# Attention scores on 64-row tiles of the array: one head pair per tile, masks moved to GpSimd, one ring of four banks

## What is computed

```
x = x + LN(attn(LN(x)))          # 16 heads of 8 features, causal, ALiBi bias
    scores = q k^T * 8**-0.5 + slope[h] * (i - j);  scores = where(i >= j, scores, -inf)
    out = softmax(scores) @ v @ Wo + bo
x = x + LN(ffn(LN(x)))
    ffn(x): x = x + LN1(attn(x))  # the same size, no mask, no bias
            x = x + LN2(moe(x))   # 8 experts, 2 chosen of each token, hidden 512, gelu
```

## Time and profile before

| | us |
|---|---|
| median of 3 runs | 2289.57 |
| lowest and highest run | 2287.91, 2292.93 |
| profiled execution, first to last instruction | 2287.5 |

### The profile page before, as it was taken

One profiled execution on the slowest core, in us unless ns is written; L12 is line 12 of the kernel. 1 busy time (PEld: TensorE's weight loads), 2 busy tenths in 40 slices (PEclk: granted clock), 3 DMA queues, 4 the chain that ended last, 5 costly groups with the idle time before them and its releaser, 6 DMA issues. The chain is left out here.

```text
span 2287.5 us, 41083 instructions
## 1 busy us (share of the span) xinstructions
PE 2102.9 (92%) x11100; PEld 1223.1 (53%) x11100; DVE 1671.8 (73%) x3157; ACT 1373.5 (60%) x2647; POOL 977.3 (43%) x744
## 2 busy tenths in 40 slices
PE   5899999999999679999999999999993999999996
PEld 4455555555554534555555555555531666666664
DVE  5766667666672787777777777778822899998986
ACT  4266566666666616666666666666672655555654
POOL 3665464553610355333333333342002466565554
PEclk7799999999999679999999999999996999999998
DMA  2000000000000300000000000000001100000000
GB/s 59 1 2 1 3 1 1 2 2 1 1 1 2 110 0 1 2 1 1 2 1 1 2 1 1 1 1 1 1 1 61 51 19 19 2 19 19 19 10 10
DMA packets 27508, 24.96 MB, mean 11 GB/s; under 512 B 2409, under 2 KB 21110, under 8 KB 27282
## 3 DMA queue, kind: packets, MB, share of 16 engines
q1 hardware_dynamic: 26400, 21.91, 3.2%
q10 hardware_dynamic: 882, 0.36, 0.1%
HBM read 13.87 MB, written 6.29 MB: 9 GB/s over the span
## 5 line engine op out<-in xcount | busy, mean ns | idle before, releaser
L466 DVE TENSOR_REDUCE at_mx<-at_a 128x1 f32<-128x512 f32 (+3 forms) x1632 | 1010.8, 675 | 358.7 <-PE at_a L333 249.5
L415 ACT ACTIVATE at_probs<-at_b 128x512 f32<-128x512 f32 (+3 forms) x1792 | 888.6, 558 | 474.0 <-PE at_b L360 292.7
L333 PE MATMUL at_a<-at_km,at_fq 128*128 128x512 f32 (+1 forms) x1632 | 704.8, 439 | 20.4 <-DVE at_mx L466 9.8
L360 PE MATMUL at_b<-at_fqm,at_km 128*128 128x512 f32 (+3 forms) x1792 | 710.8, 404 | 11.4 <-ACT at_probs L415 7.6
L333 PEld LDWEIGHTS at_a<-at_km,at_fq 128*128 128x128 f32 x1632 | 316.3, 194 | 290.0 <-DVE at_mx L466 224.4
L360 PEld LDWEIGHTS at_b<-at_fqm,at_km 128*128 128x128 f32 x1792 | 339.8, 191 | 205.5 <-ACT at_probs L415 120.3
L378 PE MATMUL at_pv<-at_probs,at_vst 128*32 128x512 f32 (+3 forms) x3584 | 437.9, 561 | 1.5 <-ACT at_probs L415 1.5
L556 POOL TENSOR_TENSOR at_hi<-at_u,split_sign 128x512 fp32r<-128x512 f32 x120 | 124.9, 1041 | 441.1 <-ACT at_u L404 306.5
L1172 ACT ACTIVATE t_hid<-t_bank_h,b1t 128x512 f32<-128x512 f32 x256 | 174.3, 689 | 195.9 <-DVE t_hid_lo L1306 113.1
L1306 DVE TENSOR_TENSOR t_hid_lo<-t_hid,t_hid_hi 128x512 fp32r<-128x512 f32 x256 | 225.6, 917 | 15.0 <-ACT t_hid_hi L1179 11.8
L569 POOL TENSOR_TENSOR at_km<-at_fk,head_mask 128x2048 fp32r<-128x2048 f32 x60 | 216.1, 3602 | 11.2 <-POOL at_fk L567 11.0
(11 more groups left out here) (211 smaller groups left out, 2410.3 us busy)
## 6 DMA issues: line engine op xcount, KB each, us to landing
t_raw<-L_ffn_W SPq DMA_DIRECT2D x16, 256.0 KB, 3.1
x_first<-L_attn_x SPq DMA_DIRECT2D x4, 512.0 KB, 7.3
second_x_in<-L_attn_x SPq DMA_DIRECT2D x8, 256.0 KB, 3.1
kept<-second_joined SPq DMA_DIRECT2D x8, 256.0 KB, 2.6
kept_u<-second_normed SPq DMA_DIRECT2D x8, 256.0 KB, 2.0
t_heads_in<-tokens SPq DMA_DIRECT2D x8, 256.0 KB, 2.6
t_u_in<-kept_u SPq DMA_DIRECT2D x8, 256.0 KB, 3.1
t_x_in<-kept SPq DMA_DIRECT2D x8, 256.0 KB, 3.1
```

The lines of the kernel that those rows point to most:

```text
L333: mm = pe.matmul(scores, fq[g][:, qt * P:(qt + 1) * P], km[g][:, heads[0]:heads[0] + k, kh * HALF:kh * HALF + w], start=True, stop=not dia ...
L360: mm = pe.matmul(out[:, 0:w], km[g][:, j, kt * P:(kt + 1) * P], fqm[g % 2][:, q0:q0 + w], start=True, stop=not diagonal)
L415: act.activation(probs[(t % 2) * GH + j][:, 0:w], b_bank[n % 3][:, 0:w], ACT.Exp).then_inc(exp_done, 1)
L466: dve.tensor_reduce(mx[:, kh, qt, heads[0]:heads[0] + k], a_bank[n % 3][:, 0:k * w].rearrange("p (k w) -> p k w", k=k), AX.X, ALU.max).the ...
```

## The change

- Keys: `km` has two layers instead of four. Rows 0 to 63 belong to heads 0 and 1, rows 64 to 127 to heads 2 and 3; layer j % 2 has only head j's 32 rows nonzero, in its half. The tiles are cleared once in the first block; after that `fk` (now two buffers) is copied in by four DMAs of 32 partitions x 512 columns a half, issued by SP. The product with `head_mask` goes.
- `a` and `b` matmuls contract over the 64 rows of the head's pair. `b` takes the heads in the order 0, 2, 1, 3, and so do chunks of one head; chunks have at most two heads (in at1 40 chunks a slot instead of 38; at2 keeps 64).
- The causal mask: for `a` two matmuls of 64 rows each (`half_ident`, `half_mask`) instead of one of 128; for `b` none, POOL sets the upper triangle of the four exponentials to zero after the fact (`affine_select`), and `pv` waits for it (`masked`).
- Order of a step: first `b`, all `a`, the other three `b`, then as before. `lead` is 3; `pv` is that of the quad two before.
- Banks: `a`, `proj`, `otr` and `mtr` share one ring of four banks in the order of the list; `b` keeps three and `pv` one. `probs` holds four quads instead of two.

```diff
+RING = ("a", "proj", "otr", "mtr")
+A_BANKS = 4
+B_BANKS = 3
+PROBS = 4
+B_HEADS = (0, 2, 1, 3)
+PAIR = 2 * HW
...
-                per = max(1, HALF // n)
-                per = 4 if per >= 4 else per
-                for j in range(0, GH, per):
+                per = 2 if n <= HALF // 2 else 1
+                for j in (0, 2) if per == 2 else (0, 2, 1, 3):
...
-        self.lead = 2
-        a_steps = nq - 4
+        self.lead = 3
+        a_steps = nq - 2 - self.lead
...
-            out += self.interleave(bs, ass)
+            out += bs[:1] + ass + bs[1:]
...
-            dp, p = (ds, q - 1) if q else (0, self.nq - 1)
+            dp, p = (0, i + 1) if i + 1 < self.nq else (1, 0)
...
-                        scores = out[:, 0:k * w].rearrange("p (k w) -> p k w", k=k)
-                        mm = pe.matmul(scores, fq[g][:, qt * P:(qt + 1) * P],
-                                       km[g][:, heads[0]:heads[0] + k, kh * HALF:kh * HALF + w],
+                        scores = misc[:, 0:k * w].rearrange("p (k w) -> p k w", k=k)
+                        rows = slice(PAIR * (heads[0] // 2), PAIR * (heads[0] // 2 + 1))
+                        first = heads[0] % 2
+                        mm = pe.matmul(scores, fq[g][rows, qt * P:(qt + 1) * P],
+                                       km[g][rows, first:first + k, kh * HALF:kh * HALF + w],
                                        start=True, stop=not diagonal)
                         if diagonal:
-                            mm = pe.matmul(scores[:, :, w - P:w], ident16[:, :],
-                                           causal_mask[:, None, :].broadcast_to([P, k, P]),
-                                           start=False, stop=True)
+                            for i in range(2):
+                                mm = pe.matmul(scores[:, :, w - P:w], half_ident[rows, i, :],
+                                               half_mask[rows, i, None, :].broadcast_to([PAIR, k, P]),
+                                               start=False, stop=(i == 1))
...
-                        out = b_bank[n % 3]
-                        mm = pe.matmul(out[:, 0:w], km[g][:, j, kt * P:(kt + 1) * P],
-                                       fqm[g % 2][:, q0:q0 + w], start=True, stop=not diagonal)
-                        if diagonal:
-                            mm = pe.matmul(out[:, 0:P], causal_mask[:, :], ident16[:, :],
-                                           start=False, stop=True)
+                        out = b_bank[n % B_BANKS]
+                        rows = slice(PAIR * (j // 2), PAIR * (j // 2 + 1))
+                        mm = pe.matmul(out[:, 0:w], km[g][rows, j % 2, kt * P:(kt + 1) * P],
+                                       fqm[g % 2][rows, q0:q0 + w], start=True, stop=True)
...
+                        if n in plan.diagonals:
+                            done(pe, masked, len(plan.diagonals), s, plan.diagonals.index(n))
...
+                    if what == "b" and n % GH == GH - 1 and n // GH in plan.diagonals:
+                        await_(exp_done, NB, s, n)
+                        block_ = probs[n // GH % PROBS][:, :, 0:P]
+                        pool.affine_select(block_, block_, [[0, GH], [1, P]], ALU.is_ge, 0.0, base=0,
+                                           channel_multiplier=-1).then_inc(masked, 1)
...
+                    if m:
+                        await_(keys_spread[h], KEYS, s - 1, KEYS - 1)
+                    dst = fk[h][:, :] if m else fq[g][:, half]
+                    pool.tensor_tensor(dst, part[:, :], un[:, :], ALU.add).then_inc(split_done, 1)
...
+        @block.sync
+        def _(sp):
...
+                    if ds == 3 and n == 0:
+                        done(sp, b_made, NB, s - 4, NB - 1)
+                    done(sp, split_done, 4, s, n)
+                    for j in range(GH):
+                        rows = slice(HW * j, HW * (j + 1))
+                        sp.dma_start(km[g][rows, j % 2, h * HALF:(h + 1) * HALF].bitcast(F32),
+                                     fk[h][rows, :].bitcast(F32)).then_inc(keys_spread[h], 16)
```

More of the change, by code:

```diff
@@ L76, in __init__ @@
                 self.quads.append((qh, kt))
+        self.diagonals = [t for t, (qh, kt) in enumerate(self.quads) if causal and kt * P >= qh * HALF]
         self.na = len(self.chunks)
@@ L135, in body, with places @@
         return out
+    def places(self, steps):
+        order = [step for step in steps if step[0] in RING]
+        return {step: place for place, step in enumerate(order)}
     def prologue(self):
@@ L247, in attention @@
         dve_step = sem("dve_step")
+        keys_spread = [sem(f"keys_spread{i}") for i in range(2)]
         v_staged = sem("v_staged")
@@ L288, in _, with emit, bank_free @@
                 pe.sem_inc(semaphore, per)
-            def emit(steps, s0, b0, g0):
-                prologue = steps[0][0] == "proj" and steps[0][1] == 0
-                before = None if prologue else ("otr", -1, 1)
+            def emit(steps, s0, b0, g0, places, before):
+                prologue = places is in_prologue
+                held = list(places)
+                emitted = (set(steps), set(before))
+                def bank_free(step):
+                    place = places[step] - A_BANKS
+                    while True:
+                        back = 0 if place >= 0 else 1
+                        if prologue and back:
+                            return
+                        what, ds, n = held[place]
+                        if held[place] in emitted[back]:
+                            break
+                        place -= A_BANKS
+                    s = s0 + (ds - back)
+                    if what == "a":
+                        done(pe, a_read, NA, s, n)
+                    elif what == "proj":
+                        done(pe, proj_read, 4, s, n)
+                    elif what == "otr":
+                        done(pe, o_done, 2, s, n)
+                    else:
+                        done(pe, fqm_made, 2, s, n)
                 for what, ds, n in steps:
                     s = s0 + ds
[L295 to L307, removed]
+                    if what in RING:
+                        bank_free((what, ds, n))
+                        misc = a_bank[places[what, ds, n] % A_BANKS]
                     if what == "proj":
@@ L1516, in gpsimd @@
                 pool.memset(row3[:, :, :, :, :], 0.0).then_inc(zeroed, 1)
+                for i in range(2):
+                    pool.memset(km[i][:, :, :].bitcast(F32), 0.0).then_inc(cleared, 1)
                 pool.wait_ge(zeroed, 1)
```

144 lines of the change are left out of this document (76 added, 68 removed).

## The result

The changed kernel takes 2211.99 us in the median (2207.67 to 2218.02, 4 runs), the kernel before 2288.74 beside it (2287.1 to 2292.93): a ratio of 0.9668, 95% interval 0.9647 to 0.9689. That is 77 us less, where 219 were forecast. The time lies above the forecast's range of 1975 to 2182 us. The page after: span, busy time, the slices of PE and of its clock, three of its groups, and the DMA that is new.

What follows compares the result with a forecast made beforehand. PE was taken to bound both attention stages. From 2287.5 us, 94.5 (at2), 112.5 (at1), 10 (starts) and 3 (last slots) came off, giving 2067.5, so 2070 us as the median; range 1975 to 2182 us.

Steps and rivals of the forecast that it cites:

- Overlap of the halves: Score matmuls on 64 rows: two row halves overlap fully, 13.1 us a slot less in at2, 7.6 in at1.
- Loads one after another: Rival for score matmuls: halves overlap in streaming, but each waits for its own weight load; 2160 us, chance 0.17.
- doesn't do what it says: Rival: a half of the rows runs no sooner than the whole array; 2287 us, no change, chance 0.08.
- drains: Rival for score matmuls: going between halves empties the array, 0.09 us each, no overlap remains; 2495 us, chance 0.05.
- Who is late next in at2: At2 slots: PE (42.0 us) and DVE (42.5) become equal and coupled through four banks; 48.1 us a slot, gain 94.5.
- the forecast's chain of 2.54 us: At2, from a step's last chunk to the next step's first chunk result; leaves DVE idle 0.15 us a step.
- Its last sentence: At2: a chain through the banks longer than 2.54 us would break the sum even with overlap; DVE's idle time shows it.
- at1: Causal attention stage: PE still sets the slot, 33.5 us instead of 41.0, gain 112.5 us.
- POOL: At1 triangle selections: 1.3 us each, covered, 23.1 us of POOL a slot; rival at 3.6 us each 2182, chance 0.10.
- Starts and last slots: Stage starts lose two key products on DVE, 10 us less; last slots lose 3 us over 26 steps.
- the bare 0.32: Last slots: time from fourth score to values falls from 0.43 to 0.32 us, 3 us less over 26 steps.
- The granted clock is no case of its own: PE's clock in the last slot: 1.00 of 2.4 GHz though PE waits there; no longer waits expected, so no separate rival.

Runs made afterwards that it cites:

- the later turns: Both turns of the row maxima one step later in the slot, against the kernel with values in halves (2131.98 us): 2160.48 us, ratio 0.9449.
- the added matmuls: Changed kernel with extra half-row matmuls into idle banks in the last slot's steps: 2204.98 us with two from the fifth quad on, 2207.19 with four from the first step.

## Where the forecast failed, and what of it was right

- **Overlap of the halves: right.** Five starts in 0.6 us, loads in pairs, no price for going from one half to the other. "Loads one after another", "doesn't do what it says" and "drains" all fall with the timeline after and with the 245 us by which the halved values are slower without overlap. By the Trainium skill, TensorEngine Tiling (Array Packing), "Key Properties", a change of the tile alone doesn't drain TensorE; the prediction could compare that for columns only, and for rows this trace agrees (1311.03, both halves start together). The streaming gain was put at 7.6 and 13.1 us a slot; where nothing hides it, it is 6.4 and 11.1.
- **Who is late next in at2: the step that failed.** The forecast put 48.1 us a slot, from DVE's work plus 0.15 us of idle time a step (2.55 us); measured 52.45. Two terms were missing.
  - The wait of the fourth "b" for its bank, put at nothing. In the forecast's chain of 2.54 us the last chunk of a step is followed by the values after 0.23 + 0.46 + 0.09 = 0.78 us. Measured it is 1.13 (1311.59 to 1312.72): 0.70 until the fourth "b", whose bank ACT has to read first, and 0.43 until the values. The next step's first chunk starts with its first "b", which gives 0.22 back. That makes 2.69 us for each step, 16 x 0.14 = 2.2 us a slot. With four banks for "b" the wait is gone, and a shorter exponential shortens it by as much.
  - The uneven chunks, which make long steps that short ones don't repay: 2.2 us, the gain of the even ones.

48.1 + 2.2 + 2.2 = 52.5. With both mended the slot took the forecast's 48.1, but in an order of steps that the forecast had not summed, so this equality is in part luck. The chain was in the earlier trace rows, and the forecast used it for the last slot alone, though a burst of "b" on a faster PE meets the same three banks in every slot. Its last sentence looked for a longer chain through the ring and DVE, not through ACT. The Trainium skill, TensorEngine Tiling (Array Packing), "PSUM Bottleneck", says that tiling quickens TensorE but not the emptying of PSUM. That pointed the right way; but here the banks' readers bound by their delay before they were full (DVE 82% busy). The prediction also read a plain step of the kernel before as 2.9 us, where it takes 3.05; as its sums start from whole slots, this changed none of them.

- **at1: right in kind, too low.** 33.5 us forecast, 36.0 in a regular slot, 36.8 with the boundaries. The forecast let PE work without a pause, and took no wait into account. PE had none before. Over three regular slots of the changed kernel it has, first its busy time and then one of the waits:

```profile
133.50:241.40 107.90, 101.99 (x790) 53.21 (x788) 81.37 (x150) 71.92 (x162) 56.17 (x64) 1.00 0.07 16
```

```profile
PE at_a L381 <- DVE at_mpad L513: 3.1, 3, 1.0
```

So 2.0 of the 2.5 us that are missing are idle time, half of it before the turns, which wait for the padded maxima, and most of the rest before "b". Moving the fourth matmul and shortening the exponential gain 0.9 and 0.8 us in a regular slot of at1, so the chain through ACT costs something there too; the even chunks and the halved values bring nothing (36.4 both). Which count the last 0.5 us belong to is open.

- **POOL: right.** 0.634 us a selection, half of the 1.3 taken; the value matmuls waited for it once, 1.7 us, and 6.2 us of idle time of their loads in at1 ended with it (25 times). The 64 KB DMA landed in 2.0 us in the median, inside the 2.7 taken.
- **Starts and last slots: wrong.** -13 us forecast. The last slot of at1 gave +12. The last slot of at2 took 52.7 us, against 52.3 before: its step is 2.61 us against 2.62, for the values still start 0.42 us after the fourth "b" (1602.25 to 1602.67), and not the bare 0.32.

The starts gave 0.7 us (first merge at 89.1 against 89.8) and 1.0 (115.7 against 116.7), of 5 each. With full rows and the same code for the keys they gave 5.5 and 6.6, so DVE's shorter start is real, and most likely a slower PE took it back: over the 30 us before at2's first merge the clock is 0.50 in the changed kernel and 1.00 with full rows, in this order:

```profile
776.00:806.00 30.00, 30.00 (x59) 14.60 (x58) 26.04 (x43) 3.44 (x5) 17.50 (x16) 0.50 0.07 18
```

```profile
808.00:838.00 30.00, 26.52 (x69) 11.79 (x69) 30.00 (x51) 4.53 (x7) 21.38 (x19) 1.00 0.11 27
```

"The granted clock is no case of its own" failed: it looked at the waits before the change, and not at what PE does once two matmuls share the time of one.

Sum of the misses against the forecast's 2067.5: 50 us in at1 (552.7 - 502.5), 65 in at2 (786.7 - 721.5), and 24 in starts and last slots (-13 forecast, +12.0 - 1.1 measured): 139, with 138.5 to explain (2206.0 - 2067.5).

## What to carry over

Before counting what a faster engine saves, walk one step from the first result to the last bank that must be free again, and take that as the floor of every step; look for it where the kernel already runs without its main bound, as in a last slot. Where steps have different limits, sum the larger of the limits step by step, not the totals. If a change makes an engine faster and the time hardly moves, spread its consumers' bursts (here half of the values between two pairs of scores) before giving up the change. And before a sum of waits is believed, look where its gaps stand: a load queue that is idle while the matmuls before it stream waits for nothing.

## What the runs showed of the hardware

The clock granted to PE was not the same for two forms of the same work. At the start of at1, where DVE holds up PE, the window from 70 to 110 us reads, in the changed kernel, in the one with full rows and the change's order, and in the two with the values in halves (scores on half rows, then on full rows), in this order:

```profile
70.00:110.00 40.00, 37.07 (x150) 20.15 (x149) 25.74 (x50) 12.02 (x24) 24.01 (x23) 0.63 0.10 25
```

```profile
70.00:110.00 40.00, 32.63 (x172) 19.15 (x174) 29.03 (x54) 14.23 (x29) 26.88 (x27) 1.00 0.11 27
```

```profile
70.00:110.00 40.00, 38.77 (x150) 21.52 (x153) 27.68 (x52) 11.14 (x20) 22.24 (x21) 0.58 0.08 20
```

```profile
70.00:110.00 40.00, 33.25 (x169) 18.68 (x168) 29.61 (x55) 11.59 (x22) 27.91 (x27) 0.93 0.11 27
```

With half rows the clock stays mostly at 1.2 GHz there, with full rows at 2.4 GHz. All nine kernels with half rows lie between 0.50 and 0.67 in this window, the two with full rows at 0.93 and 1.00, the kernel before at 0.88. In the last slot of at1, 0.61 on the mean stands against 1.00 with full rows. But half rows alone don't bring the clock down: in the last slot of at2 it is 1.00 in every kernel, and in that of at1 it is 1.00 with four banks for "b" and with the later turns. At 1.2 GHz a block of values takes 1.94 us (675.26 in the changed kernel) instead of 1.07. So part of what the overlap saves is given back in the clock: regular slots alone gain 102 us over full rows in the change's order (6.8 x 15), the whole kernel 79; the starts and the last slot of at1 make up the difference. Whether the rows in use or the time in which PE stands still decides was not separated; the added matmuls changed both.
